# A ternary feed-forward stage rebuilt as one block: normalisation per chunk, all up products first, down products one chunk behind

## What is computed

```
h = silu(z W1' * s1) * (z W2' * s2)      # 512 wide
h = gelu(h H1' * t1)                     # 512 x 512
h = gelu(h H2' * t2)                     # 512 x 512
x = x + 0.5 * (h W3' * s3)               # back to 128
```

## Time and profile before

| what | value |
|---|---|
| time, median of 3 runs | 2705.04 us (2702.67 to 2705.21) |
| the profiled execution, its own time | 2699.5 us |
| its span in the profile | 2697.7 us |
| mean granted PE clock | 0.903 of full |
| instructions | 43512 |
| ternary stages, first statistics to last write of x | from 1010.0, 1675.1, 2210.0 and 2522.5 us, 167.5 to 169.3 us each |

### The profile page before, as it was taken

One profiled execution on the slowest core, in us unless ns is written; L12 is line 12 of the kernel. 1 busy time (PEld: TensorE's weight loads), 2 busy tenths in 40 slices (PEclk: granted clock), 3 DMA queues, 4 the chain that ended last, 5 costly groups with the idle time before them and its releaser, 6 DMA issues. The chain is left out here.

```text
span 2697.7 us, 43512 instructions
## 1 busy us (share of the span) xinstructions
PE 2206.9 (82%) x17001; PEld 1205.0 (45%) x17001; DVE 1544.6 (57%) x2836; ACT 1167.2 (43%) x2024; POOL 355.4 (13%) x539
## 2 busy tenths in 40 slices
PE   3988986978988979988999997995659569960598
PEld 1665664655655654442222222443437444430344
DVE  4985985558968961147788783015734770148510
ACT  2774772446746732223777775221234222230121
POOL 2331331113413400000000000000010000013000
PEclk9999998989999999985999999997766789985799
DMA  3000000010000000001100000000000100000000
GB/s 127 4 6 3 4 6 7 2 46 1 6 5 1 6 13 16 0 26 58 28 28 20 27 11 10 0 0 4 1 20 18 45 8 0 0 0 0 0 0 16
DMA packets 28448, 38.60 MB, mean 14 GB/s; under 512 B 17026, under 2 KB 19330, under 8 KB 27618
## 3 DMA queue, kind: packets, MB, share of 16 engines
q1 hardware_dynamic: 28114, 35.03, 4.1%
q0 software_dynamic: 144, 0.96, 0.2%
HBM read 27.88 MB, written 4.46 MB: 12 GB/s over the span
## 5 line engine op out<-in xcount | busy, mean ns | idle before, releaser
L1985 DVE TENSOR_REDUCE fa_top<-psum 128x1 f32<-128x1024 f32 x256 | 304.5, 1220 | 85.3 <-PE psum L1930 84.5
L1974 ACT ACTIVATE fa_prob<-psum 128x512 f32<-128x512 f32 x512 | 278.7, 597 | 118.2 <-PE psum L1943 117.2
L472 DVE TENSOR_TENSOR scaled<-psum,area_b 128x512 f32<-128x512 f32 x16 | 11.1, 691 | 472.6 <-PE psum L437 472.6
L430 PE MATMUL psum<-hidden_a,area_b 128*128 128x512 f32 x512 | 221.0, 592 | 0.0
L430 PE MATMUL psum<-hidden_b,area_b 128*128 128x512 f32 x512 | 221.0, 592 | 0.0
L1943 PE MATMUL psum<-fa_stack_q,fa_stack_k 74*128 74x512 bf16 x512 | 199.5, 393 | 10.9 <-ACT fa_prob L1974 5.1
L1930 PE MATMUL psum<-fa_stack_k,fa_stack_q 72*128 72x512 bf16 x512 | 204.4, 409 | 3.8 <-DVE fa_top L1985 2.9
L620 POOL TENSOR_TENSOR turn_a<-turn_a,turn_b 128x1024 f32<-128x1024 f32 x64 | 151.0, 2360 | 297.3 <-DVE turn_b L838 297.3
L637 PE MATMUL psum<-area_a,zt 128*128 128x512 f32 x256 | 135.9, 656 | 29.6 <-ACT k_t L769 14.8
L430 PEld LDWEIGHTS psum<-hidden_a,area_b 128*128 128x128 f32 x512 | 97.3, 190 | 122.4 <-issue 122.4
L430 PEld LDWEIGHTS psum<-hidden_b,area_b 128*128 128x128 f32 x512 | 97.3, 190 | 122.4 <-issue 122.4
(11 more groups left out here) (331 smaller groups left out, 4375.5 us busy)
## 6 DMA issues: line engine op xcount, KB each, us to landing
area_b<-in_L_ffn SPq DMA_DIRECT2D x2, 2888.0 KB, 9.7
fa_stack_q<-fa_parts_dram SPq DMA_DIRECT2D x144, 32.0 KB
fa_stack_k<-fa_parts_dram SPq DMA_DIRECT2D x144, 32.0 KB
area_a<-in_L_ffn SPq DMA_DIRECT2D x1, 4402.0 KB, 12.9
fa_parts_dram<-fa_prob SPq DMA_DIRECT2D x12, 256.0 KB, 2.5
moved_halves<-y SPq DMA_DIRECT2D x16, 127.0 KB
area_b<-in_L_attn SPq DMA_DIRECT2D x1, 1880.5 KB, 16.7
area_a<-in_L_attn SPq DMA_DIRECT2D x1, 1538.0 KB, 6.2
```

What stands on the lines that cost most here:

```text
L430: last = nc.tensor.matmul(psum[:, 4 + n % 2, :], w(name)[:, k * TF_HID + m * P:k * TF_HID + (m + 1) * P], src[:, c, k, :], start=(k == 0), ...
L1974: nc.scalar.activation(prob[:, (2 * s + j) % RING, half * CHUNK:(half + 1) * CHUNK], psum[:, 4 + n % 2, :], ACT.Exp, scale=float(D) ** -0. ...
L1985: nc.vector.tensor_reduce(top[:, g % 2, j, t:t + 1], psum[:, 2 * j:2 * j + 2, :].rearrange("p a n -> p (a n)"), AX.X, ALU.max, negate=True ...
```

## The change

The ternary stage becomes one block without a loop. A new class does the normalisation chunk by chunk inside it; the transposes use the banks of the down products (6 and 7). PE transposes chunk c+1 ahead of the up products of chunk c. All 16 up pairs come first, then the first hidden product of all four chunks, then the second, with the down products of chunk c-1 behind the second hidden products of chunk c. DVE issues the statistics of chunks 0 and 1, their normalisation, then statistics and normalisation of chunks 2 and 3, then all gates, then all additions. A tile's own signal is gone: one signal per chunk is given after the fourth tile. hidden_a and hidden_b hold four chunks in place of two. ACT loads the silu table by an explicit instruction at the stage's start. The counts of products, transposes, activations and DVE operations on x stay; statistics and powers come in four groups in place of two.

```diff
--- before.py
+++ after.py
@@ -48,6 +48,7 @@
+SILU = 18
@@ -276,6 +277,66 @@
+class ChunkNorm:
+    def __init__(self, core, source, out, eps):
+        self.core, self.source, self.out, self.eps = core, source, out, eps
+        (self.counted, self.merged, self.spread_ready, self.rstd_ready, self.normed, self.turned, self.taken) = (core.sem(n) for n in (
+            "half_stats", "moments", "spread_ready", "rstd_ready", "tile_normalised", "bank_transposed", "bank_evacuated"))
+    def tiles(self, c):
+        return range(c * PER_CHUNK, (c + 1) * PER_CHUNK)
+    def span(self, c):
+        return slice(c * PER_CHUNK, (c + 1) * PER_CHUNK)
+    def dve_stats(self, dve, c):
+        core, nc = self.core, self.core.nc
+        for i in self.tiles(c):
+            last = nc.vector.bn_stats(core.stats[:, i, :], self.source[:, i, :])
+        last.then_inc(self.counted.handle, 1)
+        dve.wait_ge(*self.counted.at(c + 1))
+        for i in self.tiles(c):
+            last = nc.vector.bn_aggr(core.moments[:, i, :], core.stats[:, i, :])
+        last.then_inc(self.merged.handle, 1)
+        dve.wait_ge(*self.merged.at(c + 1))
+        nc.vector.tensor_scalar(core.spread[:, self.span(c)], core.moments[:, self.span(c), 1], self.eps, None,
+                                ALU.add).then_inc(self.spread_ready.handle, 1)
+    def pool_root(self, pool, c):
+        core, nc = self.core, self.core.nc
+        pool.wait_ge(*self.spread_ready.at(c + 1))
+        nc.gpsimd.tensor_tensor(core.rstd[:, self.span(c)], core.spread[:, self.span(c)], core.minus_half[:, self.span(c)],
+                                ALU.pow).then_inc(self.rstd_ready.handle, 1)
+    def dve_normalise(self, dve, c):
+        core, nc = self.core, self.core.nc
+        dve.wait_ge(*self.rstd_ready.at(c + 1))
+        for i in self.tiles(c):
+            last = nc.vector.tensor_scalar(self.out[:, i, :], self.source[:, i, :], core.moments[:, i, 0:1], core.rstd[:, i:i + 1],
+                                           ALU.subtract, ALU.mult)
+        last.then_inc(self.normed.handle, 1)
+    def pe_turn(self, pe, c, bank):
+        core, nc = self.core, self.core.nc
+        pe.wait_ge(*self.normed.at(c + 1))
+        if c >= 2:
+            pe.wait_ge(*self.taken.at(c - 1))
+        for j, i in enumerate(self.tiles(c)):
+            last = nc.tensor.transpose(bank[:, j * P:(j + 1) * P], self.out[:, i, :], core.ident[:])
+        last.then_inc(self.turned.handle, 1)
+    def act_take(self, act, c, bank):
+        core, nc = self.core, self.core.nc
+        act.wait_ge(*self.turned.at(c + 1))
+        nc.scalar.copy(core.zt[:, c * CHUNK:(c + 1) * CHUNK], bank).then_inc(self.taken.handle, 1)
+    def close(self):
+        for tally in (self.counted, self.merged, self.spread_ready, self.rstd_ready, self.normed, self.turned, self.taken):
+            tally.done += CHUNKS
@@ -388,99 +449,141 @@
 def ternary_ffn(core, area):
     nc, psum, x, zt = core.nc, core.psum, core.x, core.zt
     w = core.weights(area, TERNARY)
-    normalise_block(core, x, core.y, 1e-5, plain(core))
-    up, silu, gated, hid, acted, low, added = (core.sem(n) for n in (
-        "up_product", "silu", "gated", "hidden_product", "gelu", "out_product", "added"))
-    chain = core.sem("vector_chain")
+    up, silu, gated, hid, acted, low, scaled_up, added = (core.sem(n) for n in (
+        "up_product", "silu", "gated", "hidden_product", "gelu", "out_product", "biased_queries", "added"))
     M = TF_PARTS
+    HIDS = M * CHUNKS
+    norm = ChunkNorm(core, x, core.y, 1e-5)
     with ExitStack() as ctx:
         sb = lambda name, shape: ctx.enter_context(nc.sbuf_tensor(core.fresh(name), shape, F32))
-        ha, hb = sb("hidden_a", [P, 2, M, CHUNK]), sb("hidden_b", [P, 2, M, CHUNK])
+        ha, hb = sb("hidden_a", [P, CHUNKS, M, CHUNK]), sb("hidden_b", [P, CHUNKS, M, CHUNK])
         gate, scaled = sb("gate", [P, 2, CHUNK]), sb("scaled", [P, PER_CHUNK, P])
+        def down_bank(c):
+            return psum[:, 6 + c % 2, :]
+        def pe_up(pe, c):
+            pe.wait_ge(*norm.taken.at(c + 1))
+            for m in range(M):
+                n = c * M + m
+                if n >= 2:
+                    pe.wait_ge(*gated.at(n - 1))
+                nc.tensor.matmul(psum[:, n % 2, :], w("w1")[:, m * P:(m + 1) * P], zt[:, c * CHUNK:(c + 1) * CHUNK], start=True, stop=True)
+                nc.tensor.matmul(psum[:, 2 + n % 2, :], w("w2")[:, m * P:(m + 1) * P], zt[:, c * CHUNK:(c + 1) * CHUNK],
+                                 start=True, stop=True).then_inc(up.handle, 1)
+        def pe_hidden(pe, step, c):
+            name, source = (("h1", ha), ("h2", hb))[step]
+            if step == 0:
+                pe.wait_ge(*gated.at((c + 1) * M))
+            else:
+                pe.wait_ge(*acted.at((c + 1) * M))
+            for m in range(M):
+                n = step * HIDS + c * M + m
+                if n >= 2:
+                    pe.wait_ge(*acted.at(n - 1))
+                for k in range(M):
+                    last = nc.tensor.matmul(psum[:, 4 + n % 2, :], w(name)[:, k * TF_HID + m * P:k * TF_HID + (m + 1) * P],
+                                            source[:, c, k, :], start=(k == 0), stop=(k == M - 1))
+                last.then_inc(hid.handle, 1)
+        def pe_down(pe, c):
+            pe.wait_ge(*acted.at(HIDS + (c + 1) * M))
+            if c >= 2:
+                pe.wait_ge(*added.at(c - 1))
+            for j in range(PER_CHUNK):
+                for k in range(M):
+                    last = nc.tensor.matmul(down_bank(c)[:, j * P:(j + 1) * P], ha[:, c, k, j * P:(j + 1) * P],
+                                            w("w3")[:, k * P:(k + 1) * P], start=(k == 0), stop=(k == M - 1))
+            last.then_inc(low.handle, 1)
+        def act_silu(act, c):
+            for m in range(M):
+                n = c * M + m
+                act.wait_ge(*up.at(n + 1))
+                if n >= 2:
+                    act.wait_ge(*gated.at(n - 1))
+                nc.scalar.activation(gate[:, n % 2, :], psum[:, n % 2, :], ACT.Silu, scale=w("s1")[:, m:m + 1]).then_inc(silu.handle, 1)
+        def act_gelu(act, step, c):
+            out, scale = ((hb, "t1"), (ha, "t2"))[step]
+            for m in range(M):
+                n = step * HIDS + c * M + m
+                act.wait_ge(*hid.at(n + 1))
+                nc.scalar.activation(out[:, c, m, :], psum[:, 4 + n % 2, :], ACT.Gelu, scale=w(scale)[:, m:m + 1]).then_inc(acted.handle, 1)
+        def dve_gate(dve, c):
+            for m in range(M):
+                n = c * M + m
+                dve.wait_ge(*silu.at(n + 1))
+                nc.vector.scalar_tensor_tensor(out=ha[:, c, m, :], in0=psum[:, 2 + n % 2, :], scalar=w("s2")[:, m:m + 1],
+                                               in1=gate[:, n % 2, :], op0=ALU.mult, op1=ALU.mult).then_inc(gated.handle, 1)
+        def dve_add(dve, c):
+            tiles = x[:, c * PER_CHUNK:(c + 1) * PER_CHUNK, :]
+            dve.wait_ge(*low.at(c + 1))
+            if c:
+                dve.wait_ge(*added.at(c))
+            nc.vector.tensor_tensor(scaled[:], down_bank(c).rearrange("p (j n) -> p j n", j=PER_CHUNK),
+                                    w("s3").unsqueeze(1).to_broadcast([P, PER_CHUNK, P]), ALU.mult).then_inc(scaled_up.handle, 1)
+            dve.wait_ge(*scaled_up.at(c + 1))
+            nc.vector.scalar_tensor_tensor(out=tiles, in0=scaled[:], scalar=0.5, in1=tiles, op0=ALU.mult, op1=ALU.add).then_inc(added.handle, 1)
         with nc.Block() as block:
+            @block.gpsimd
+            def _(pool):
+                for c in range(CHUNKS):
+                    norm.pool_root(pool, c)
             @block.tensor
             def _(pe):
-                with pe.Fori(0, CHUNKS // 2) as i:
-                    for c in range(2):
-                        for m in range(M):
...
-                    pe.wait_ge(added.handle, added.done + (i + 1) * 2)
+                norm.pe_turn(pe, 0, down_bank(0))
+                for c in range(CHUNKS):
+                    if c + 1 < CHUNKS:
+                        norm.pe_turn(pe, c + 1, down_bank(c + 1))
+                    pe_up(pe, c)
+                for c in range(CHUNKS):
+                    pe_hidden(pe, 0, c)
+                pe_hidden(pe, 1, 0)
+                for c in range(1, CHUNKS):
+                    pe_hidden(pe, 1, c)
+                    pe_down(pe, c - 1)
+                pe_down(pe, CHUNKS - 1)
             @block.scalar
             def _(act):
-                with act.Fori(0, CHUNKS // 2) as i:
-                    for n in range(2 * M):
-                        act.wait_ge(up.handle, up.done + i * 2 * M + n + 1)
...
-                                                     scale=w(scale)[:, m:m + 1]).then_inc(acted.handle, 1)
+                nc.scalar.add_instruction(mybir.InstLoadActFuncSet(
```

(52 more changed lines are left out.)

38 lines of the change are left out of this document (removed).

## The result

The changed kernel took 2674.05 us (median of 4 runs, 2665.08 to 2676.92) against 2703.86 (4 runs, 2700.67 to 2705.21): ratio 0.9884, 95% interval 0.9867 to 0.9901, 1.2% faster. The forecast was 2684.8 with a range of 2678 to 2693. One execution of the kernel before, measured beside the last experiments, took 4192.11 us at a mean granted clock of 0.764, where all others took 2699 to 2714; it is left out of every ratio.

A forecast was written before the change was run, and what follows sets the result against it. PE's product stream was taken to bound each pass, leaving only heads and turns to win. Gains of 15.2 and 8.5 less 3.5 us gave 20.2, so 2705.0 became 2684.8 us, range 2678 to 2693.

The forecast's parts named there:

- The head: Each ternary stage's start, first statistics to third up pair: four heads shrink from 60.8 us to 11.4 each, 15.2 us gained.
- The turn: Between the two passes of a ternary stage: PE's wait for additions and the jump vanish, 8.5 us gained.
- The transposes in the stream: Transposes of chunks 2 and 3 now stand among the up products, 0.44 us each, 3.5 us lost.
- At nothing: Parts costed at zero, among them down products one chunk behind, additions beside products, table loads and shared banks.
- the bridge from the profiled execution to the median: Step from profile to measured time: median taken as 5.5 us above the profiled execution's 2699.5 us, so 2705.0.
- the 60.8 us of the old heads: Old time from first statistics to third up pair, four stages together: 16.25, 14.16, 14.30 and 16.11 us.
- the clock stays low longer: Rival: first two up pairs of every stage run at half speed, third pair at 13.4 us; 2692.8 us; chance 0.12.
- Straight code: Rival: fetching the loop-free code makes PE wait 3.7 us a stage, no gain, about 2700 to 2705; chance 0.04.
- Gates stop holding PE: Rival: waits for gates among the up pairs vanish, 1.0 us a stage, 4 more in all, 2681 us; chance 0.08.

The follow-up runs named there:

- e4: Changed kernel's chunked normalisation, but the old order of passes with PE waiting for both additions at the turn, written out without a loop; 2678.62 us, ratio 0.9892.
- e2: Kernel before with its two passes written out without a loop and PE's wait for the additions at the turn removed; 2694.31 us, ratio 0.9953.
- e3: Changed kernel's main block and order of products, but normalisation as the separate block of before; 2694.26 us, ratio 0.9944.
- e10: Changed kernel with all four down products behind all second hidden products, instead of one chunk behind; 2671.84 us, ratio 0.9879.
- e12: As e11, with the first two up pairs ahead of chunk 1's transposes and normalisation of chunks 2 and 3 between gates; 2665.98 us, ratio 0.9857.
- e1: Changed kernel once more, unaltered, against the kernel before; 2676.77 us, ratio 0.9888.
- e9: Changed kernel a third time, unaltered, against the kernel before; 2670.83 us, ratio 0.9875.
- e15: Changed kernel with two throwaway products on PE between the up and hidden products of each ternary stage; 2680.42 us, ratio 0.9908.
- e16: Changed kernel with four throwaway products on PE between the up and hidden products of each ternary stage; 2688.96 us, ratio 0.9946.
- e8: Changed kernel with the gates of the first two up pairs ahead of chunk 3's normalisation on DVE; 2667.91 us, ratio 0.9866.
- e11: As e8, with four throwaway products on PE at each ternary stage's start; 2667.24 us, ratio 0.9862.

## Why the prediction was right in direction and short in size

- **The head, against the first profile: right in mechanism, a little mis-sized.** First up product 6.12 (6.3 forecast), first gate 10.12 (10.3), third pair at 10.92, 10.91, 11.43 and 10.92, 44.2 in all against 45.6: 16.6 us gained in place of 15.2. I had put the clock's half speed at two heads; all four began with it, but it decided only one, as DVE's queue covers it in the others.
- **The turn: 8.5 forecast, 9.6 measured.** From the first hidden product to the last write's start, the two passes and the turn took 64.36 + 63.14 = 127.50 us in the fourth stage before and 125.09 after: 2.41 a stage. The experiments split it. From the first hidden product to the second pass's first up product it is 64.36 us before, 63.75 in e4 (the wait, but no loop) and 62.07 in e2 (neither): 1.68 for the wait and 0.61 for the jump and its register work. The last 0.12 go at the loop's end. The one fall of the clock behind the turn, 1.6 us, I did not see: I read only that PE idles 2.12 us, not what the grant did behind it.
- **The transposes in the stream: 3.5 lost by forecast, 2.2 measured as a net.** 14 up pairs took 24.97 us before and 25.53 with two groups of transposes, 0.56 a stage. e3 has the new order without the transposes:

```profile
1034.53 1.12 PE L473 MATMUL psum<-zt,area_b 128*128 128x512 f32 x2
...
1059.35 1.02 PE L488 MATMUL psum<-hidden_a,area_b 128*128 128x512 f32 x2
```

  That is 24.82 us, so the transposes themselves cost 0.71 a stage, 2.8 in all, and the written-out loop gives back about 0.1 a stage.
- **At nothing: right** for the down products (e10) and the order (e3 against e2).
- These make 16.6 + 9.6 + 1.6 - 2.2 = 25.6, the 25.5 of the first pair of profiles. Four terms erred to the same side by 1.1 to 1.6 us. With these alone the time would have been inside the range.
- **The step that failed is the bridge from the profiled execution to the median, and with it the 60.8 us of the old heads.** I added 5.5 us and otherwise took the profile's clock losses as those of every run ("as two of four heads began slow"). From first statistics to the third pair the four old heads took 60.8 us together in the first profile, but 63.7, 66.0 and 66.1 in the three later ones. The mean is 64.2, so the head's term is 64.2 - 44.2 = 20.0 us, not 15.2. The ternary stages as a whole took 675.1 to 675.9 us in the three later profiles, 672.2 in the first. The four mean 674.7, and 674.7 - 646.6 = 28.1 us. The new head lost the same in all profiles of it (161.5 to 162.1 a stage), since DVE's queue decides in three heads of four and the third stage's was slow each time: in the ternary stages the change removes not only work but most of the spread. Some 2.5 of the "5.5 us above" were the very time that the change takes away.
- All executions up to e12: 60 of before have a mean of 2704.6 us, 12 of the changed kernel (with e1 and e9) 2673.6, 31 us apart, so some 3 us lie outside the ternary stages. About 1 us is the way out of a stage (from the last write's start to the next block's first statistics 1.62 us before, 1.38 after, at the first stage). The profiles show where the rest is: from the second ternary stage's last write to the third's first statistics the four profiles of before took 366.7, 373.0, 372.4 and 372.2 us, the three of the changed kernel 369.0, 366.5 and 366.4. The first profile of before was the favourable one here too. Why those untouched stages run shorter behind the changed one is open. e15 and e16 speak against a large dependence on when they begin, and can't exclude one of this size.
- **The rivals.** Of "the clock stays low longer" half came to pass: the first pair ran at half clock in all twelve heads of three profiles. But the grant returned during the first or second pair, and the third pair came 10.9 to 11.4 us behind the start, not 13.4. Straight code cost nothing that shows. "Gates stop holding PE" is the 0.1 a stage above.
- By the rule of the Trainium skill that transposes do not count as PE activity (TensorE: Matmul & The Clock Gate, Part 4), every head would meet its first products at half clock. All twelve heads of the changed kernel did, and 13 of 16 of before; in the other three the grant came back with nothing but transposes on PE (the second head in the earlier trace rows is one), so the rule does not hold here as it stands. The rival's time of 2692.8 did not come out. No run tested the rule by itself.

## What to carry to other kernels

When a change removes idle time of TensorE, count the slow products behind that idle time too, and take them from several profiles: one execution shows one draw of the clock. Where another engine's queue covers the slow products, as DVE's did in the new heads, they cost nothing. If profile and median of before differ, ask whether the difference sits in what the change removes before carrying it over as a constant. A stage's head is best shortened by ordering each engine's queue so that the first consumer is not behind work that is needed later, and by keeping PE busy until its first real product (e8, e11 and e12).

## What the runs showed of the hardware that I had not expected

The identical head lost between nothing and 3 us to the clock from run to run: third pair of the third stage at 14.30, 17.24, 17.23 and 17.31 us in four executions of the same kernel. A wait of about 2 us was followed by a stretch at half clock at two of 16 turns and not at the other 14. Throwaway products of 3.4 us on an otherwise idle PE were worth more than they cost: ternary stages of 641.5 us in place of 645.3.
